# Attention stage of a decoder layer: the third quarter of a slot's outputs is divided on VectorE behind the negation of the maxima, and the next input's moments come last

## What is computed

```python
x = x + attn(layernorm(x), Wq, bq, Wk, bk, Wv, bv, Wo, bo)
x = x + xattn(layernorm(x), ctx, mask, ...)   # scores = where(mask == 0, 1e-09, scores)
x = x + ffn(layernorm(x), W_fc, ln_w, ln_b, W_proj)

def attn(x):                                   # xattn: K and V from ctx
    Q, K, V = proj(Wq, bq), proj(Wk, bk), proj(Wv, bv)     # 16 heads of 16
    scores = einsum('bhqd,bhkd->bhqk', Q, K) / sqrt(16)
    out = einsum('bhqk,bhkd->bhqd', softmax(scores), V)
    return out @ Wo.T + bo
```

## Time and profile before

| | before |
|---|---|
| median of 3 runs | 2350.62 us |
| the profiled execution, own time | 2349.46 us |
| its span | 2347.5 us |
| busy share PE, DVE, ACT, POOL | 93%, 82%, 68%, 45% |
| attention slots | about 27 to 1760 us of the span |

### The profile page before, as it was taken

How to read it: one execution, slowest core, us unless ns; L and a number is a source line. 1 busy time by engine, 2 the same in 40 slices (tenths; PEclk the granted TensorE clock), 3 DMA queues, 4 the chain that set the end, 5 groups by cost and what they waited for, 6 DMA issues and landing times.

```text
span 2347.5 us, 70177 instructions
## 1 busy us (share of the span) xinstructions
PE 2171.9 (93%) x29001; PEld 1444.0 (62%) x29001; DVE 1933.6 (82%) x3903; ACT 1593.7 (68%) x2351; POOL 1048.8 (45%) x849
## 2 busy tenths in 40 slices
PE   4689999999999999999999999999977999999998
PEld 2365666566656665666566656665554777777776
DVE  6788888888888888888888888887754887887877
ACT  4477766666667666666666666666545778788786
POOL 3245344534443444344434444453214555545543
PEclk8899999999999999999999999999998999999999
DMA  6577666677766667766666667676422333333332
GB/s 172 139 167 166 149 144 154 156 157 158 152 154 150 146 152 158 160 155 156 147 156 145 151 160 156 156 177 141 98 69 63 100 88 82 105 80 89 99 81 63
DMA packets 477595, 314.14 MB, mean 134 GB/s; under 512 B 292368, under 2 KB 427408, under 8 KB 477328
## 3 DMA queue, kind: packets, MB, share of 16 engines
q1 hardware_dynamic: 474224, 309.95, 56.3%
q10 hardware_dynamic: 3104, 0.34, 0.1%
HBM read 72.69 MB, written 51.38 MB: 53 GB/s over the span
## 4 chain that ended last, share of the span: by engine, by line
PE 65%; DVE 18%; issue 7%; ACT 7%; DMA 1%; SPq 1%; POOL 1%; ACTq 0%; DVEq 0%; POOLq 0%
PE product_bank L1162 14%; PE ybk L1512 10%; PE hbk L1538 9%; PE out_bank L1138 7%; PE tbk L1526 5%; PE score_bank L1085 4%; PE product_bank L1169 4%; ACT prob L850 4%; DVE out_bank L982 4%; DVE odd_mx L948 4%; PE score_bank L1104 3%; PE exp_bank L1123 3%; PE exp_bank L1085 3%; PE exp_bank L1223 3%; DVE att L997 2%
## 5 line engine op out<-in xcount | busy, mean ns | idle before, releaser
L850 ACT ACTIVATE prob<-exp_bank 128x1024 f32<-128x1024 f32 x508 | 518.5, 1021 | 258.1 <-PE exp_bank L1123 250.1
L764 POOL TENSOR_TENSOR xs<-xn,xs 128x1024 f16<-128x1024 f32 x64 | 138.8, 2169 | 624.1 <-ACT xs L874 624.1
L948 DVE TENSOR_REDUCE even_mx<-score_bank 128x8 f32<-128x1024 f32 x256 | 310.6, 1213 | 92.1 <-PE score_bank L1104 92.1
L948 DVE TENSOR_REDUCE odd_mx<-score_bank 128x8 f32<-128x1024 f32 x256 | 310.3, 1212 | 79.7 <-PE score_bank L1104 79.7
L840 ACT ACTIVATE qk<-product_bank,bcol 128x512 f16<-128x512 f32 x256 | 175.6, 687 | 219.9 <-PE product_bank L1162 209.9
L1496 DVE SCALAR_TENSOR_TENSOR ghl<-tbk,lnwc,ghl 128x512 f16<-128x512 f32 x256 | 188.0, 735 | 100.2 <-ACT ghl L1427 100.1
L1538 PE MATMUL hbk<-wfcT,ffn_xhl 128*128 128x512 f16 x1024 | 264.7, 382 | 6.1 <-ACT hid L1433 3.3
L1512 PE MATMUL ybk<-wpT,ghl 128*128 128x256 f16 x2048 | 260.5, 273 | 0.8 <-DVE ffn_y L1481 0.7
L1512 PEld LDWEIGHTS ybk<-wpT,ghl 128*128 128x128 f16 x2048 | 197.8, 98 | 66.0 <-DVE ghl L1496 0.9
L1427 ACT ACTIVATE ghl<-tbk,lnwc 128x512 f16<-128x512 f32 x256 | 174.1, 681 | 68.2 <-PE tbk L1526 68.2
L954 DVE SCALAR_TENSOR_TENSOR qk<-product_bank,bcol,qk 128x512 f16<-128x512 f32 x256 | 184.4, 741 | 29.1 <-ACT qk L840 29.1
(11 more groups left out here) (175 smaller groups left out, 4392.3 us busy)
## 6 DMA issues: line engine op xcount, KB each, us to landing
even_stk<-qk SPq DMA_DIRECT2D x384, 128.0 KB, 2.7
odd_stk<-qk SPq DMA_DIRECT2D x384, 128.0 KB, 2.8
x_scratch<-xn SPq DMA_DIRECT2D x64, 512.0 KB, 4.7
srcs<-in_x SPq DMA_DIRECT2D x32, 512.0 KB, 5.4
ctx_in<-in_ctx SPq DMA_DIRECT2D x32, 512.0 KB, 4.7
srcs<-x_scratch SPq DMA_DIRECT2D x32, 512.0 KB, 5.6
ffn_src<-x_scratch SPq DMA_DIRECT2D x32, 512.0 KB, 3.9
out<-ffn_y SPq DMA_DIRECT2D x32, 512.0 KB, 3.8
```

The lines of the kernel that those rows point to most:

```text
L764: nc.gpsimd.tensor_tensor(out, src, hi, ALU.subtract).then_inc(lo_ready, 1)
L850: act.activation(prob[:, p % 3], (sbank if s.max is None and p % 2 else ebank)[:, :, :], ACT.Exp, scale=EXP_SCALE).then_inc(b.exp_done, 1)
L948: dve.tensor_reduce(a.mx[:, g * H:(g + 1) * H].rearrange("p (r e j) -> p r e j", r=2, e=2)[:, :, eight], sbank[:, :, :].rearrange("p r (j ...
```

## The change

Two things move in VectorE's list, at the end of each slot. `outputs(b, s.exp, 2)` goes from ahead of `maximum(7)` to behind `negate`; `moments`, which came between `negate` and `masked_arguments`, comes last. Nothing is added or removed, and no other engine's list changes.

```diff
@@ dve_slot
             turn_att(b, s.exp, 0)
             maximum(6)
             more(6)
-            outputs(b, s.exp, 2)
             maximum(7)
             negate()
+            outputs(b, s.exp, 2)
+            masked_arguments()
             if not late:
                 moments(b, s.mom)
-            masked_arguments()
```

## The result

The changed kernel takes 2382.38 us (median of 4 runs, 2377.30 to 2385.49) against 2350.85 us for the kernel before: a ratio of 1.0134, with a 95% interval of 1.0117 to 1.0150. It is slower by 31.5 us. The profiled execution took 2377.30 us, its span 2375.1 us, with the same 70177 instructions.

A forecast was written before the change was run, and what follows sets the result against it. TensorE and VectorE were taken to bound the kernel together, within half a microsecond of each other in every slot. Self slots 17.7, cross slots 13.5 and ends 3 sum to 34.2 us slower: 2384.8 us, range 2370 to 2396.

The forecast's parts named there:

- the second wait: Self slot's end: TensorE's mask product for `scores(1)` must also wait for `maximum(0)`, raising the shift from 0.57 to 0.68 us.
- The pair of slots: Sign in the trace: a self and a cross slot together should last 52.0 + 1.2 us.
- The self slot: VectorE idles 0.92 us ahead of `maximum(7)`; TensorE comes 0.68 later in each of 26 self slots, 17.7 us.
- The cross slot: End of 26 cross slots: `maximum(7)` to `tile(0)` grows, nothing is bought; 0.52 us each, 13.5 us.
- the meeting: Cross slot's end: L962 meets GpSimd's L764 on shared SBUF ports; the next step follows about 0.05 us later.
- The early slots: Slots 1 to 5: 0.77 us lost each in slots 2 and 3, less in the others, 3 us.
- The late slots: Slots 59 to 63: idling 2.27 us for `weighted(3)` swallows the 1.78 that moves: 0; slot 58 about 0.
- Rival A: Faster: VectorE's slack ahead of `tile(0)` is larger, TensorE keeps its 0.43 in 26 slots, 2339.4 us; chance 0.06.
- Rival C: Only one kind of slot pays: the cross slot's idle pieces hide all of the 1.42, 2371.3 us; chance 0.11.
- Rival B: A lock: in cross slots L962 loses its turn to GpSimd's deviations, 1.3 us more each, 2419 us; chance 0.06.

The follow-up runs named there:

- stats_ahead: The changed kernel with, from slot 6 on, three of the four statistics instructions of `moments` put ahead of `maximum(7)`: 2344.34 us, ratio 0.9972.
- cross_only: The changed kernel with the new order in cross slots alone and the old order elsewhere: 2363.15 us, ratio 1.0045.
- moments_last: The changed kernel with `outputs(2)` back ahead of `maximum(7)` and `moments` still last: 2359.28 us, ratio 1.0033.
- before_late_counts: The kernel before with L962 alone moved behind `outputs(3)`: 2346.34 us, ratio 0.9979.
- outputs_only: The changed kernel with `moments` back ahead of `masked_arguments` and `outputs(2)` still behind the negation: 2384.86 us, ratio 1.0133.

## Why the prediction was right, and where it was off

**The forecast** was 2384.8 us, the result 2382.38. The mechanism was the one forecast, and the named signs of it are in the trace: the idle piece ahead of `maximum(7)` ended by L1104 (0.86 and 1.35 for 0.9 and 1.3), no wait of L1204, a wait for L954 (0.92 for about 1.0, and in cross slots 0.34 for about 0.5), the second wait (0.10 for 0.11), no idle piece ahead of L962. The pair of slots took 1.1 more, for 1.2. One sign did not come: a self slot from its negation to the next was to grow by 0.5 from 24.45, and it took 26.08, while the cross slot went from 27.57 to 27.05. The negation is itself what moved in the self slots, so only the pair can be read that way. By its parts the forecast was less exact than by its sum: the self slots cost about 1 us more than counted and the cross slots 3 less.

**The self slot** was counted at 0.68 and costs 0.72. The experiment with self slots alone gave 18.9 us with the early slots, for 17.7 + 3. The sum held because VectorE's stretch had no gap before, so a gap put in at one end comes out at the other.

**The cross slot** was counted at 0.52 and costs 0.40, 10.4 us in place of 13.5. The term that was mis-sized is the stretch from `maximum(7)` to `tile(0)`: 7.83 and 0.05 for the meeting, and it is 7.77. Two errors lie in it, one against the other. The steps overlap by a few hundredths more when one follows the other without a wait (0.13 for `masked_arguments` instead of 0.19, 1.20 for the last part of `masked_values` instead of 1.27). The meeting was priced too low: the next step follows L962 by 0.41, and 0.33 was counted, 0.28 and 0.05. The 0.28 was no undisturbed L962 either, since there it was already waiting for GpSimd's L798; undisturbed it is followed after 0.13. So the sum held 0.20 for the meeting, of which it named 0.05, and it is 0.28 to 0.29. Without it the stretch was counted at 7.68 and takes 7.48. For the same reason the 0.40 that the prediction gives as L962's own duration is that of a meeting; alone it takes 0.26.

**The early slots** were counted at 0.77 each in slots 2 and 3: 23.81 for 23.09, 0.72. Slots 1 to 5 together cost 2.9, for 3.

**The late slots** were counted at nothing. Slots 59 and 60 take 0.2 more each (31.93 for 31.73): L962 takes 1.65 there for 1.45 and 1.40, a meeting again.

**Rival A** (TensorE keeps its 0.43) did not happen, but `stats_ahead` shows that 0.23 of it is there to be had once the gap is filled. **Rival C** (cross slots free) fell: `cross_only` costs 11.7 us. It was nearer than it looked, though: the idle pieces and the closer steps hide all but 0.12 of what moved, and the meeting is the rest. **Rival B** (the meeting) is the more instructive miss. It happened in `moments_last`, where it costs 0.40 in a cross slot, and in a milder form in the changed kernel, 0.29; both are more than the 0.05 of the sum and less than the 1.3 of the rival, because in slots 6 to 60 of both traces L962 ended 0.12 to 0.13 behind the end of one GpSimd instruction, L764, and waited for no further one (in slot 30 of the changed kernel GpSimd's power L807, 1.02 us long, was still to come). The Trainium skill's rule (SBUF — State Buffer, "SBUF: two separate sides"), that the loser waits for the whole instruction, is what L962 shows here: in `moments_last` it takes 1.14 us beside an L764 of 1.16, and 0.26 in all 32 places of `before_late_counts`.

What the rival turned on, L962 coming just as L764 ends, is the case in `outputs_only`, in slot 30 as in the others. VectorE and GpSimd there:

```profile
872.34 0.30 DVE L962 TENSOR_TENSOR ue<-ew,cntL 128x64 f32<-128x64 f32 x1 [0.32 <-ACT ew L908]
```

```profile
871.18 1.17 POOL L764 TENSOR_TENSOR ahl<-attT,ahl 128x512 f16<-128x512 f32 x1
872.31 0.21 POOL L803 TENSOR_TENSOR odd_ve<-odd_mv,eps 128x4 f32<-128x4 f32 x1
```

L962 starts 0.02 before L764 ends and ends 0.12 behind the end of L803, the next one. It lost 0.04 us and not 1.3; whether L803 went first is not shown.

**Left open.** The scatter of the runs. The traces give part of it a place: slot 4 takes 23.81 us in the changed kernel and 25.38 in `outputs_only`, whose order in that slot is the same; slot 60 takes 31.69 in the kernel before and 33.55 in `cross_only`, and slot 62 is at 31.6 to 34.0 in the various traces. These steps of 1.5 us or more come in some executions and not in others. What sets them off was not tried. Nor is it shown what made the two executions of 7494 and 7844 us.

## What to carry to other kernels

Before a step on an in-order engine is moved out of the way of a wait, look at what the engine would do in its place: a step that seems to delay a result may be filling the time in which its successor's input is being made. Where the freed time can be filled by work with no tie to either side, the move can pay: the same order with three small instructions in the gap was 38 us faster than without them, and about 28 with the meetings set aside. And the place of a short instruction with two inputs in SBUF should be chosen against GpSimd's timeline as well as its own engine's: 0.38 us later in its slot (2.90 behind the negation instead of 2.53), it took 1.14 us instead of 0.40.

## What the runs showed of the hardware that was not expected

An instruction of 0.26 us (L962) had a median of 0.40 in the kernel before, 0.53 in the changed one and 1.14 in `moments_last`, by nothing but when it fell beside GpSimd's instructions. The kernel before paid for this about 5 us (2351.5 to 2352.1 against 2346.34 with the instruction elsewhere; the traces place 2.7 of them), with no row of waits that names it: the wait is booked as the instruction's own duration, and only the spread between minimum and maximum of one form shows it.
